# The causal mask of the second attention pass as a select by GpSimd on the probabilities, in place of TensorE's mask matmuls

## The reference

```python
q = _rope(q, ROPE_THETA)
k = _rope(k, ROPE_THETA)
scores = jnp.einsum('bhqd,bhkd->bhqk', q, k) * D ** (-0.5)
causal = jnp.tril(jnp.ones((T, T), dtype=bool))
scores = jnp.where(causal[None, None], scores, -jnp.inf)
weights = jax.nn.softmax(scores, axis=-1)
out = jnp.einsum('bhqk,bhkd->bhqd', weights, v)
```

## Time and profile before

| | us |
|---|---|
| median of 3 runs | 2505.49 (2499.48 to 2506.9) |
| profiled execution, its own time | 2505.8 |
| its span, first to last instruction | 2503.7 |
| PE busy | 1802.5 |
| DVE busy | 1556.4 |
| ACT busy | 1099.7 |
| POOL busy | 520.9 |

### The profile page before, as it was taken

How to read it: one execution, slowest core, us unless ns; L and a number is a source line. 1 busy time by engine, 2 the same in 40 slices (tenths; PEclk the granted TensorE clock), 3 DMA queues, 4 the chain that set the end, 5 groups by cost and what they waited for, 6 DMA issues and landing times. The chain is left out here.

```text
span 2503.7 us, 54131 instructions
## 1 busy us (share of the span) xinstructions
PE 1802.5 (72%) x17852; PEld 1289.2 (51%) x17853; DVE 1556.4 (62%) x2850; ACT 1099.7 (44%) x2152; POOL 520.9 (21%) x462
## 2 busy tenths in 40 slices
PE   5994888755879999993089599989874320599930
PEld 2773555644769999993045234434343320477730
DVE  3653766574555566554478699989837962355555
ACT  2652555453544444441055177777763422233310
POOL 0442000024800000004646200000001337100046
PEclk8996999955679999997589599999997555799975
DMA  4334553024721111114323422322100125222254
GB/s 135 114 110 140 159 152 117 16 85 152 242 75 46 50 46 50 46 46 141 111 93 138 133 70 70 104 70 70 49 16 30 34 85 195 94 80 84 82 170 134
DMA packets 194208, 240.08 MB, mean 96 GB/s; under 512 B 24884, under 2 KB 153556, under 8 KB 193540
## 3 DMA queue, kind: packets, MB, share of 16 engines
q1 hardware_dynamic: 176152, 183.92, 23.5%
q0 software_dynamic: 17696, 54.02, 6.3%
q10 hardware_dynamic: 204, 0.05, 0.0%
HBM read 133.10 MB, written 103.84 MB: 95 GB/s over the span
## 5 line engine op out<-in xcount | busy, mean ns | idle before, releaser
L827 DVE TENSOR_REDUCE a_mx<-a_pmx 128x4 f32<-128x512 f32 (+1 forms) x448 | 457.6, 1057 | 88.1 <-PE a_pmx L778 68.0
L875 ACT ACTIVATE a_probs<-a_pst 128x512 f32<-128x512 f32 (+2 forms) x832 | 421.9, 562 | 202.3 <-PE a_pst L794 167.2
L1797 PE MATMUL m_ph<-m_zh,m_w 128*128 128x256 f16 x2808 | 322.0, 274 | 18.7 <-DVE m_zh L1875 18.5
L1811 PE MATMUL m_py<-m_w,m_zh 128*128 x2808 | 319.4, 273 | 0.1
L1797 PEld LDWEIGHTS m_ph<-m_zh,m_w 128*128 x2808 | 272.3, 98 | 60.1 <-issue 26.1
L1934 POOL DMA_INDIRECT m_got<-m_ys_d,m_slot x128 | 127.1, 993 | 771.9 <-issue 767.9
L1811 PEld LDWEIGHTS m_py<-m_w,m_zh 128*128 128x128 f16 x2808 | 268.3, 98 | 35.6 <-issue 2.0
L807 PE MATMUL a_pacc<-a_probs,a_V 128*32 128x256 f32 (+4 forms) x3456 | 246.8, 368 | 0.7 <-ACT a_probs L875 0.3
L1881 DVE CAST m_zh<-x_res 128x512 f16<-128x512 f32 x234 | 99.6, 426 | 207.1 <-ACT x_res L1847 103.6
L1845 ACT ACTIVATE x_res<-m_ph,m_b,m_s 128x256 f32<-128x256 f32 x312 | 157.2, 561 | 126.3 <-PE m_ph L1797 117.1
L766 PE MATMUL a_pmx<-a_Ks,a_Qs 48*128 48x192 f16 (+4 forms) x1280 | 166.7, 309 | 51.4 <-DMA a_V<-v_d 35.5
(11 more groups left out here) (207 smaller groups left out, 2959.7 us busy)
## 6 DMA issues: line engine op xcount, KB each, us to landing
xs_d<-a_zero POOLq DMA_DIRECT2D x26, 768.0 KB, 4.8
m_zh<-xs_d SPq DMA_DIRECT2D x78, 256.0 KB, 2.7
m_ys_d<-x_res SPq DMA_DIRECT2D x78, 256.0 KB, 2.2
v_d<-p_vt SPq DMA_DIRECT2D x16, 1024.0 KB, 4.6
parts_d<-p_part SPq DMA_DIRECT2D x64, 256.0 KB, 2.6
a_V<-v_d SPq DMA_DIRECT2D x32, 512.0 KB, 3.9
a_Qs<-parts_d SPq DMA_DIRECT2D x192, 64.0 KB, 2.7
a_Ks<-parts_d SPq DMA_DIRECT2D x192, 64.0 KB, 2.4
```

The costliest lines, as they stand in the source:

```text
L827: nc.vector.tensor_reduce(mx[:, part, :, ps[0]:ps[0] + len(ps), i], src, AX.X, ALU.max).then_inc(m_done, 1)
L875: nc.scalar.activation(probs[:, (hg * NV + g) % NGB, 2 * a + u % 2, 0:w], pst[:, bank(hg, u), 0:w], ACT.Exp, scale=HD ** -0.5).then_inc(ex ...
L1797: mm = nc.tensor.matmul(ph[:, (G * par + g) % 4, q * ROWS:(q + 1) * ROWS], self.w1[:, bass.ds(e, 1), c, wp, m * P:(m + 1) * P].rearrange(" ...
L1811: mm = nc.tensor.matmul(py[:, a, 0:D], hh[:, par, m, hp, a * P:(a + 1) * P], self.w2[:, bass.ds(e, 1), m, wp, :].rearrange("p a n -> p (a ...
```

## The change

The mask matmuls of the second pass are left out in layer 1. The exponentials therefore run on unmasked scores in the diagonal blocks, and afterwards GpSimd selects, in place on `probs`, the entries whose query is not before the key and writes 0.0 elsewhere: one `affine_select` for each of the 10 masked pairs, over both of its banks. It covers 256 elements in each partition for a pair with one diagonal block in a bank (pairs 0, 1, 13, 14) and 512 for the other six. `pe_pv` of a masked group waits for the selects too. The DMAs that write zeros keep their number and are issued one by one after a step's selects. Layer 0 and the first pass keep their masks.

```diff
+            cuts, cut_done = [n for n, (_, _, p) in enumerate(pairs) if layer and p[1]], sem("cut_done")
...
-                                              Qs[par][ROW2 * r:ROW2 * r + KAUG, p, q0:q1], start=at == 0, stop=copies == 0, skip_group_check=True)
-                for b in range(nb):
+                                              Qs[par][ROW2 * r:ROW2 * r + KAUG, p, q0:q1], start=at == 0, stop=layer == 1 or copies == 0, skip_group_check=True)
+                for b in range(0 if layer else nb):
...
                 pe.wait_ge(exp_done, NE * s + 2 * last_pair[v] + 2)
+                if [n for n in cuts if pairs[n][0] == v]:
+                    pe.wait_ge(cut_done, len(cuts) * s + len([n for n in cuts if pairs[n][0] <= v]))
...
-                    for j in range(XT * ROWS // (A * P)):
-
-                        pool.wait_ge(pv_done, NX * (j + 1))
-                        dst = self.xs_d[layer][j * A * P:(j + 1) * A * P, :].rearrange("(a p) n -> p a n", p=P)
-                        pool.dma_start(dst, zero[:, :].unsqueeze(1).broadcast_to([P, A, 2 * D])).then_inc(self.zero_out, 16)
+                    fill = nc.gpsimd.to_reg(0.0) if layer else None
+                    for s in range(STEPS):
+                        for n in cuts:
+                            g, a, (_, copies, step, _) = pairs[n]
+                            pool.wait_ge(exp_done, NE * s + 2 * n + 2)
+                            tile = probs[:, (s * NV + g) % NGB, 2 * a:2 * a + 2, 0:copies * step].rearrange("q r (n c) -> q r n c", c=step)[:, :, :, 0:P]
+                            nc.gpsimd.affine_select(tile, tile, [[0, 2], [0, copies], [1, P]], ALU.is_ge, fill, base=0, channel_multiplier=-1).then_inc(cut_done, 1)
+                        if 1 <= s <= XT * ROWS // (A * P):
+
+                            pool.wait_ge(pv_done, NX * s)
+                            dst = self.xs_d[layer][(s - 1) * A * P:s * A * P, :].rearrange("(a p) n -> p a n", p=P)
+                            pool.dma_start(dst, zero[:, :].unsqueeze(1).broadcast_to([P, A, 2 * D])).then_inc(self.zero_out, 16)
```

## The result

The changed kernel takes 2514.49 us in the median of 7 runs (2509.65 to 2516.86), against 2505.49 before: 1.0041 times as long (95% interval 1.0026 to 1.0057), which is 10 us (6.5 to 14.3); the two medians are 9.0 apart. It is slower, as forecast, but by 10 us where 22.5 were forecast; 2514.5 lies near the low end of the range.

The account below looks back on a forecast made before the run. No engine alone was taken as the bound; TensorE and VectorE take turns, with waits deciding. Steady steps 15.7, steps 0 and 8 1.5, steps 14 and 15 5.1: 22.3 us on 2505.8, so 2528; range 2511 to 2547.

Parts of the forecast that it names:

- The mechanism and the places: Masked PVs wait for GpSimd's select: 0.46 us late at group 8, 0.06 at group 0, 0.79 at group 1.
- the price of the select, S: Duration of one GpSimd select, taken as 0.90 us for 512 elements and 0.54 for 256.
- my own sum for a steady step: Net delays at the PVs of groups 8, 0 and 1 after mask savings: 1.31 us, 15.7 over 12 steps.
- Steps 0 and 8: Steps starting late on TensorE, with more cover at group 1: 1.5 us lost together, an estimate.
- Steps 14 and 15: Last steps, few first-pass units left between scores and PV, so cover shrinks: 5.1 us lost together.
- Cover: Gap from last exponential to PV: 0.38 us at group 8, 0.24 at group 1; groups 2, 7, 9 lose nothing.
- Hand-overs: Around each select: 0.08 us from ScalarE to GpSimd and 0.05 from GpSimd to TensorE, added to S.
- What the masks give: TensorE's mask time, 1.0 us a step; only masks of pairs 16, 0 and 3 credited: 0.12, 0.07, 0.12.
- GpSimd's queue and the DMA: Ten selects, 7.6 us a step, plus 0.83 for the DMA fit GpSimd's time; 2 us and more to spare.
- Both rivals on GpSimd: Far dearer select makes GpSimd the bound, 2600 to 2745 us, chance 0.07; DMA holds it 4.8 us, 2567, chance 0.04.
- that of the clock: Less busy TensorE drops to 1.2 GHz; a step there some 15 us longer; chance 0.01 that it shows.
- my low bound: Total loss with the select at the conversion's price (0.61, 0.40): 0.59 us a step, 10.8 in all, 2516.5.

Follow-up runs that it names:

- the short select: Changed kernel with each select covering only one of the two banks, the other bank left unmasked: 2503.85 us, ratio 0.9991 to the kernel before.
- the double one: Changed kernel with a second, same-size select on an unread tile ahead of each select: 2543.54 us, ratio 1.0143 to the kernel before.

## Why the prediction was wrong

The mechanism and the places were right; the term that failed is the price of the select, S, for which no row stood. I wrote "I take the middle, 0.90 for 512 and 0.54 for 256", between a one-input conversion and a two-input product. The chip gave 0.637 and 0.419. The conversion's line (0.18 us and 0.83 ns an element) says 0.61 and 0.40, so index and comparison cost 0.03 us at most beyond it, and the nearest row was the answer, not a middle towards a row with two inputs. With the measured price my own sum for a steady step is 0.19 at group 8 (0.76 - 0.38 - 0.12 - 0.07), -0.06 at group 0 and 0.52 at group 1, together 0.65 in place of 1.31; measured is 0.69 (26.92 less 26.23). The experiments that set the price to other values lie near the same sum: 26.32 with the short select, where it gives some 26.4, and 28.47 with the double one, where it gives 2.2 us over the kernel before and 2.24 were measured.

From the first exponential of each of the 16 steps to that of the next, the terms of the sum can be read one by one. The twelve steady steps are 7.9 us longer in all, where 15.7 stood; one of them (step 11) is hardly longer at all (27.49 for 27.46), since in the kernel before ScalarE already waits 1.80 us at its end. Steps 0 and 8 are 0.15 and 2.1 longer, where 1.5 stood for both. Steps 14 and 15 are 1.5 and 1.1 longer, where 5.1 stood for both (a figure to which the terms given for it, 1.31 in each and the rest, don't add up in either reading: 4.1 or 5.0). With 0.65 for 1.31 the twelve would be 7.8, so the price accounts for the first of these; step 8 is another matter, below.

Point by point:

- *Cover.* Groups 8 and 1 named, groups 2, 7 and 9 free: shown by the timeline and by the kernel in which TensorE masks just groups 8 and 1. VectorE's idle times, forecast at 0.84 and 1.3, are 0.82 and 1.03. That the first hits with a price too high is chance, of two errors: the price was too high, and I added the net delay to the idle time, where the rows show the whole wait (0.38 and TensorE's 0.43 at group 8 are 0.81; 0.43 and 0.56 at group 1 are 0.99).
- *Hand-overs.* 0.08 and 0.05 forecast (0.08 in the sum, 0.07 in the row that it came from); 0.06 and 0.05 at the PV of group 1 measured.
- *What the masks give.* I counted 0.31 us a step. Without any mask it is 0.58. This second term was too low. I had held the masks of pairs 1, 2, 4, 13 to 15 and 17 worthless, since TensorE waits behind them for VectorE, for an exponential or for a select; the runs say otherwise. In the kernel without masks VectorE waits 0.32 us before a step's first reduction instead of 0.38, and two rows of reductions that run close behind TensorE take less time from first to last. Each in the kernel before and in the one without masks:

```profile
1566.64 3.25 DVE L827 TENSOR_REDUCE a_mx<-a_pmx 128x4 f32<-128x512 f32 x3
...
1582.85 6.10 DVE L827 TENSOR_REDUCE a_mx<-a_pmx 128x4 f32<-128x512 f32 x6
```

```profile
1567.17 3.04 DVE L831 TENSOR_REDUCE a_mx<-a_pmx 128x4 f32<-128x512 f32 x3
...
1583.14 5.87 DVE L831 TENSOR_REDUCE a_mx<-a_pmx 128x4 f32<-128x512 f32 x6
```

  That is 0.06, 0.21 (groups 0 and 1) and 0.23 us (the last pairs of the step) of the 0.58. So masks that I held worthless gave a little each, in gaps too small to stand out as waits. With selects in place the masks' worth is 0.34, close to my 0.31, since some of them only filled the cover. My sum had both the masks (0.31 for 0.58) and the waits (0.65 and 0.31, 0.96, for 1.27) about 0.3 too low, and the two cancel in its total.
- *GpSimd's queue and the DMA.* Busy 6.29 us in a step, and every select waits for ScalarE and none in a queue; the DMA holds GpSimd for 0.84 us and delays no select. Both rivals on GpSimd are out, and so is that of the clock for the steady steps, which run at 1.00. The Trainium skill's 12 cycles an element for code that branches on data (GPSIMD Engine Reference, Elementwise side-by-side cycle accounting) does not hold for this instruction, which takes 0.90 ns an element between 128 and 512. The same page of the Trainium skill gives 1.03 to 2.03 cycles for compare and select (Performance pitfalls for Q7 kernels), by which I had an estimate of 0.44 to 0.87 us for 512 elements; the trace agrees, with 0.637.
- *The edges and the total.* From the first exponential to the first copy of the next stage:

```profile
1428.43 1.09 ACT L875 ACTIVATE a_probs<-a_pst 128x512 f32<-128x512 f32 x2 [1.31 <-PE a_pst L794]
...
1856.36 1.15 ACT L1078 ACTIVATE o_at<-attn 128x512 f32<-128x512 f32 x2 [1.83 <-PEq L881]
```

```profile
1432.66 1.09 ACT L879 ACTIVATE a_probs<-a_pst 128x512 f32<-128x512 f32 x2 [1.23 <-PE a_pst L790]
...
1874.07 1.15 ACT L1089 ACTIVATE o_at<-attn 128x512 f32<-128x512 f32 x2 [1.83 <-PEq L885]
```

427.93 us before and 441.41 after: 13.5 us in these two executions. The rest of the two, which the change does not touch, differs by 4.2 us up to here and by -7.5 behind it, so that the two spans are 10.2 apart. Seven runs of the kernel before scatter by 10 us (2496.89 to 2506.94), and the 13.5 lies within the interval of the ratio. My own sum with the price of the conversion, 10.8, was my low bound; that it equals the 10 us measured is chance too, since the stage itself lost 13.5.

One thing in this stage was not in the sum: step 8, behind the branch of TensorE's loop, is 2.1 us longer. At the end of step 7 TensorE stands idle at that branch, for 3.4 us in the kernel before and 2.8 in the changed one, and within 0.8 us of the end of that idle time the granted clock falls to 0.50, the 1.2 GHz level; it stays there for 6.8 us before and for 13.65 after:

```profile
1645.40:1652.20 6.80, 6.54 (x58) 2.56 (x54) 3.69 (x5) 3.89 (x8) 0.83 (x1) 0.50 0.59 193
```

```profile
1653.02:1666.67 13.65, 12.72 (x92) 4.12 (x96) 6.65 (x8) 6.90 (x13) 2.75 (x5) 0.50 0.47 138
```

In the low stretch TensorE was busy for 0.96 of the time in the first and for 0.93 in the second, which waits at the selects too. That the waits kept the clock down longer is not shown: the kernel with two selects for one had 13.65 us too, but others with selects had 10.2 or 6.8, each in one profiled execution, and none was made to part the two. Nor does the length alone decide: step 8 is longer than the steady step by 2.2 to 2.5 us in the four kernels with 6.8 us at the low level, by 2.4 to 2.9 in the six with 10.2, and by 3.9 (changed kernel) and 3.1 in the two with 13.65.

## What to carry to other kernels

A wait that is put in front of an instruction in a strictly ordered stream costs about (time until ready) less (the cover that is left once the change is made), at each place; of the engine time freed elsewhere only what lies on the path comes off. So measure the cover at each place in the timeline first, and move to another engine only what fits under it. Here 0.24 and 0.38 us of cover stood against 0.76, and only 0.14 and 0.26 of them outlast the masks.

For an instruction without a row, the row with the same streams (here one in, one out) was the best guess in this one case, 0.61 for 0.637; take it as the value and the others as the bounds. Where one select follows the last of several producers, cut it up by producer, so that only the last piece is behind the last producer; here that took the step from 26.92 to 26.43 us.

Work saved right ahead of a wait on another engine is in part swallowed by the wait: the same mask matmuls were worth 0.58 us a step without the selects and 0.34 with them. And work moved ahead of an instruction that waits for nothing makes that instruction late.

## What the runs showed that I had not expected

The select on GpSimd is a straight line: 0.291, 0.408 to 0.419 and 0.637 us for 128, 256 and 512 elements, about as fast as a conversion (0.291 for 128, and 0.61 for 512 by its line). Two of them without a wait between start 0.59 us apart, 0.05 less than one lasts. Moving units of the first pass ahead of a long PV made the kernel before slower (26.67 for 26.23 us a step): the idle time came back behind the next PV, and ScalarE got its scores 0.43 us later.
